# First attention: each score for the row minima issued twice in a row into its bank, with the same operands

## The reference, cut to what matters

```
Q, K, V = (x @ W.T).reshape(b, h, t, d)        # a plain reshape: b=2, h=16, t=1024, d=16
scores  = einsum('bhqd,bhkd->bhqk', Q, K), masked above the diagonal
weights = softmax(scores / sqrt(d))
ctx     = einsum('bhqk,bhkd->bhqd', weights, V)
```

## Time and profile before

| | us |
|---|---|
| three runs | 1635.82, 1642.70, 1643.36 |
| median | 1642.7 |
| the profiled execution | 1639.44 |
| its span | 1637.8 |
| first attention within the span | 233.3 to some 570 |
| TensorE busy | 1281.2 (78%) |
| VectorE busy | 895.5 (55%) |
| mean granted TensorE clock | 0.87 |

### The profile page before, as it was taken

How to read it: one execution, slowest core, us unless ns; L and a number is a source line. 1 busy time by engine, 2 the same in 40 slices (tenths; PEclk the granted TensorE clock), 3 DMA queues, 4 the chain that set the end, 5 groups by cost and what they waited for, 6 DMA issues and landing times. The chain is left out here.

```text
span 1637.8 us, 22609 instructions
## 1 busy us (share of the span) xinstructions
PE 1281.2 (78%) x7428; PEld 898.7 (55%) x7428; DVE 895.5 (55%) x2331; ACT 727.6 (44%) x1668; POOL 518.6 (32%) x556
## 2 busy tenths in 40 slices
PE   2675729889899828585899999987485999999977
PEld 2564714334344327464666666666474666666656
DVE  6645538765858243244666666650244666666640
ACT  1534404554646602443555555540334555555530
POOL 0221233332422200040555555520131554445520
PEclk8787955975959959797999999998797999999998
DMA  2313196554550086202100111005102001010005
GB/s 77 118 59 114 56 97 61 60 60 51 69 52 24 27 267 181 64 14 71 37 30 29 35 37 36 27 14 161 42 26 81 23 27 46 26 46 23 17 27 154
DMA packets 133157, 101.02 MB, mean 62 GB/s; under 512 B 48240, under 2 KB 120368, under 8 KB 132784
## 3 DMA queue, kind: packets, MB, share of 16 engines
q1 hardware_dynamic: 132000, 98.53, 26.6%
q10 hardware_dynamic: 1040, 1.05, 0.2%
HBM read 56.30 MB, written 34.87 MB: 56 GB/s over the span
## 5 line engine op out<-in xcount | busy, mean ns | idle before, releaser
L748 POOL TENSOR_SCALAR a_p<-a_p,a_rl 128x128 f32<-128x128 f32 (+7 forms) x256 | 214.9, 840 | 437.1 <-DVE a_rl L690 437.0
L731 ACT ACTIVATE a_p<-psum,a_nm 128x128 f32<-128x128 f32 (+7 forms) x256 | 189.9, 742 | 193.3 <-DVE a_nm L684 192.1
L1225 ACT ACTIVATE a_pt<-psum 128x512 f32<-128x512 f32 (+3 forms) x384 | 167.1, 492 | 148.0 <-PE psum L1098 146.2
L781 PE MATMUL psum<-ident,a_p 128*128 128x128 f32 x1152 | 186.3, 279 | 56.2 <-ACT a_pt L715 35.2
L1088 PE MATMUL psum<-a_op_k,a_op_q 64*128 64x512 f32 (+3 forms) x384 | 160.7, 511 | 51.1 <-POOL a_op_k L1023 31.7
L781 PEld LDWEIGHTS psum<-ident,a_p 128*128 128x128 f32 x1152 | 130.8, 141 | 94.1 <-ACT a_pt L715 52.5
L803 PE MATMUL psum<-a_pt,v 128*64 128x256 f32 (+1 forms) x1280 | 158.9, 370 | 2.0 <-ACT a_pt L715 2.0
L684 DVE CUSTOM_DVE_ANT_0 psum<-psum,mask_a 128x128 f32<-128x128 f32 (+3 forms) x128 | 63.8, 499 | 173.3 <-PE psum L766 173.2
L1098 PE MATMUL psum<-a_op_q,a_op_k 64*128 64x512 f32 (+3 forms) x384 | 134.8, 455 | 0.0
L1088 PEld LDWEIGHTS psum<-a_op_k,a_op_q 64*128 64x128 f32 x384 | 80.1, 236 | 87.4 <-issue 31.9
L1098 PEld LDWEIGHTS psum<-a_op_q,a_op_k 64*128 64x128 f32 x384 | 73.4, 230 | 88.9 <-ACT a_pt L1225 46.3
(11 more groups left out here) (257 smaller groups left out, 2822.6 us busy)
## 6 DMA issues: line engine op xcount, KB each, us to landing
a_swap<-a_raw SPq DMA_DIRECT2D x64, 128.0 KB, 2.3
ot_d<-a_ot SPq DMA_DIRECT2D x16, 512.0 KB, 2.6
o_ot<-ot_d SPq DMA_DIRECT2D x16, 512.0 KB, 6.3
a_raw_q<-qk_d SPq DMA_DIRECT2D x48, 128.0 KB, 5.2
a_raw_k<-qk_d SPq DMA_DIRECT2D x48, 128.0 KB, 9.2
a_wf<-wf_d SPq DMA_DIRECT2D x16, 384.0 KB, 3.3
qk_d<-p_stage_h SPq DMA_DIRECT2D x8, 512.0 KB, 2.7
qk_d<-p_stage_l SPq DMA_DIRECT2D x8, 512.0 KB, 3.4
```

The source lines that it names most:

```text
L731: e.activation(s.p[:, t % NPB, 0:(i + 1) * P], C.score[t % 2][:, 0:(i + 1) * P], ACT.Exp, scale=-1.0, bias=s.nm[:, k:k + 1], accum_out=s.l ...
L748: e.tensor_scalar(s.p[:, t % NPB, 0:(i + 1) * P], s.p[:, t % NPB, 0:(i + 1) * P], s.rl[:, k:k + 1], 1.0, ALU.mult, ALU.mult).then_inc(s.no ...
L781: ins = e.transpose(C.turn[par][:, (k - k0) * P:(k - k0 + 1) * P], s.p[:, tt % NPB, k * P:(k + 1) * P], C.ident[:, :])
L1225: e.activation(pt[:, k // G0 % NPT, hd, off:HALF], bank_b("score", g, k)[:, off:HALF], ACT.Exp, scale=-1.0).then_inc(exped, 1)
```

## The change

Every A score is issued as two matmuls in a row, with the same operands, into the same bank. Each starts a new accumulation, so the second overwrites the first with the same values. The semaphore that VectorE waits for is raised by the second.

```diff
                     free_a("score", g, k)
                     k0, k1 = w * HALF, min((w + 1) * HALF, (i + 1) * P)
-                    e.matmul(bank_a("score", g, k)[:, 0:k1 - k0], q[rows(hd), hd % 2, i * P:(i + 1) * P],
-                             kk[rows(hd), hd % 2, k0:k1], start=True, stop=True).then_inc(a_scored, 1)
+                    for _ in range(2):
+                        ins = e.matmul(bank_a("score", g, k)[:, 0:k1 - k0], q[rows(hd), hd % 2, i * P:(i + 1) * P],
+                                       kk[rows(hd), hd % 2, k0:k1], start=True, stop=True)
+                    ins.then_inc(a_scored, 1)
```

## The result

The changed kernel took 1653.6 us (median of four runs, 1650.6 to 1656.1) against 1641.2 us for the kernel before in the same comparison: a ratio of 1.008, 95% interval 1.0048 to 1.0112, or some 13 us slower. The forecast was 13.6 us faster. The profiled execution after took 1650.59 us, 11.2 us more than the one before (1639.44), and this is what the following accounts for.

A forecast was written before the change was run, and what follows sets the result against it. VectorE, 28 us busy per iteration, was taken to set the pace at full clock, TensorE at half clock. Terms -15.6 + 0.5 + 1.5 = -13.6 us on 1642.7 us gave 1629 us, range 1610 to 1668 us.

The forecast's parts named there:

- What bounds the kernel now: First attention: VectorE, 28 us busy per iteration, mostly sets the pace at full clock; TensorE does where the clock is halved.
- The cost of a duplicate: Iterations at full clock: duplicates add 8.1 us of TensorE, of which 3.8 us show above iteration 6's 33.9 us.
- What it does to the stall: TensorE's wait for GpSimd at slot 34 shrinks from 2.9 us; iterations 1 to 6 run at full clock, -15.6 us.
- the 1.1 us that the clock survives: Waits of about 1.1 us for the normalisation in iterations 3, 5 and 6, without a fall of the clock.
- the prediction's factor of 1.43: Slots 0 to 23 and 36 to 47: time at half clock over full clock, 34.8 against 24.3 us.
- Iteration 0, +1.5 us: Iteration 0, starting at half clock: slower slots but perhaps an earlier clock, +1.5 us, from -1.5 to +9 us.
- The start, +0.5 us: Iteration -1, A scores alone at half clock: duplicates mostly hidden under VectorE, +0.5 us; not hidden at all, 15 us.
- R2: Rival: the clock still falls once in iterations 1, 2 and 4; +50 us, 1692 us; chance 0.12.
- R3: Rival: one or two cold stretches left, each some 15 us above the forecast; 1650 us, 1640 to 1670; chance 0.17.
- The chance of 0.24 for slower: Whole kernel: probability given to a slower result, made of R2 and most of R3.
- The second rule of the Trainium skill: Short idle times between matmul bursts make the clock swing; set aside because 64.6 us of full clock held despite waits.

The follow-up runs named there:

- e1: Changed kernel, but with the A scores of iteration -1 issued once and only those of iterations 0 to 6 twice: 1646.1 us, ratio 1.0027.
- e0: The changed kernel run again without any further edit, in a later group: 1646.0 us, ratio 1.0057 to the kernel before.
- e3: Changed kernel with the reciprocals' turn back moved from slot 34 to 40 and the normalisation from 36 to 41: 1617.9 us, ratio 0.9868.
- e5: Changed kernel with GpSimd's second reorder held back until VectorE's first cut of the minima in iteration -1: 1642.5 us, ratio 1.0049.
- e10: Kernel before with turn back at slot 44, normalisations at 45 and 16, only A scores of at most 256 columns issued twice: 1600.6 us, ratio 0.9736.

## Why the prediction was wrong

- **What bounds the kernel now**: right. The swing between iterations with a stall and iterations at half clock is what moving the turn back and its normalisation removed, for 44 us (ratio 0.9732).
- **The cost of a duplicate, 37.7 us for an iteration at full clock**: right, with some luck in the last digit, since it was the middle between 35.8 and 39.6 us. Iterations of the changed schedule without a fall and without a stall took 37.5 (e1) and 37.4 us (e0). On schedules without the waits the difference was 3.3 and 3.4 us, where 3.8 us had been forecast.
- **What it does to the stall: the step that failed.** "The stall shrinks from 2.9 us to 0.2 to 0.5 us, well below the 1.1 us that the clock survives. [...] So iterations 1 to 6 would all run at full clock". TensorE's part was right (26.7 us against 27.1). GpSimd was ready 27.7 to 28.5 us in, where 27.6 was forecast, since its operand landed late and not always at the same point (its second reorder began 23.2 to 24.2 us into the iteration, against 22.9 and 23.0 us in iterations 1 and 4 before), and the stall was 1.0 to 1.9 us. And there was no wait of 1.1 us that the clock safely survives. The waits for `normalise` in iterations 3, 5 and 6, from which that limit was read, are 1.28 us; but in iteration 0 of the same trace the clock fell 0.28 us after such a wait of 1.29 us, and in iteration 2, at 355.3, behind one of 0.72 us. In the changed kernel the stall and the normalisation's wait of 1.2 us follow each other within 3 us, and the clock fell in 14 of 18 iterations: behind the stall where it was 1.4 us or more, behind or in the second wait where it was shorter.

  Compared with 6 x 37.45 = 224.7 us, the measured 244.6 us hold 6.4 us of stalls, and the rest, some 13 us, roughly fits the 37.5 us at half clock that the profile has there (the prediction's factor of 1.43 makes 11 us of it). The gain of the clock in iterations 1 to 5 (0.72 to 0.82 before, 0.88 to 0.96 after) and the price of the duplicates, 6 x 3.5 = 21 us, all but cancelled; iteration 6, which had the full clock before, only lost (33.9 to 40.2 us).
- **Iteration 0, +1.5 us: 2.7 us.** The full clock came back earlier, as forecast (at 271.0 instead of 280.1 us), but TensorE then waited 2.80 us for GpSimd at slot 34, where it had waited 0.35 us, and the clock fell for 10.2 us. The sum had no term for this.
- **The start, +0.5 us: mis-sized, 8.0 us.** 4.6 us of it is pace: 30.4 us (e3 and e5) with no slow VectorE instruction against 25.8. VectorE is busy 25.75 us there (e3), so it waited for scores. Nearly all of it belongs to the wide duplicates: in e10, with only the narrow ones, iteration -1 took 30.1 us with a slow subtraction of 3.64 us in it. The likely reason is that a duplicate lengthens the way from a free bank to a finished score, and that the three banks hold too little work behind two short minima of 128 columns; this was argued from the timeline, not tested. The other 3.4 us are the subtraction behind the reorder, which e5 took away.
- **The rivals.** R2 (the swing stays, 1692 us) did not happen: the long stretches of half clock are gone. What happened is nearest to R3, cold stretches left; but where R3 had one or two of 15 us' worth each, there was one in every iteration from 1 to 6, 3.4 to 10.2 us long and together worth some 13 us, with the start's 7 us on top. The chance of 0.24 for slower was carried by these two. The range reached to 1668 us, so it held the time; the sign was wrong.
- **The second rule of the Trainium skill** that the prediction weighed (TensorE: Matmul & The Clock Gate, psum-queue depth-cycling: short idle times between bursts make the clock swing) was turned down for one stretch of 64.6 us. The runs agree with it more than with the dismissal: waits of 0.4 to 2.2 us for GpSimd, the shorter ones with one of 1.2 us behind them, made the clock fall again and again.

## What to carry to other kernels

Extra matmuls that only keep TensorE busy cost time of their own, here 3.3 to 3.5 us in an iteration of 32 to 34 us, and most of the clock that they hold is to be had for nothing where a wait can be moved: six slots for one transpose, with its normalisation right behind it, were worth 2.7%, the duplicates cost 0.8%. When the forecast rests on a wait that the clock survives, look through the whole trace for a fall behind a wait of that size before you trust the limit; then look at the next wait behind it, and at the scatter of the transfer that ends it. And a slower engine moves every other engine's work in time: look for what the moved work now meets.

## What the runs showed of the hardware

- A VectorE instruction of 0.17 us took 2.9 to 3.6 us when it started under a GpSimd instruction of 3.65 us that reads and writes SBUF, and ended with it. With the GpSimd instruction held back it took 0.17 us. The Trainium skill's page SBUF — State Buffer (SBUF: two separate sides) says that the two share a pair of ports under an exclusive lock, held for the whole instruction, so that the loser blocks; the timeline agrees. It was the subtraction with two SBUF inputs in some runs and the cast with one in others.
- The same wait of 1.21 us with the same work around it let the clock fall in iteration 6 of the changed kernel's first profile and left it at 1.00 in iteration 6 of its second (e0). A single wait of this size doesn't decide it.
- With every score of kind A issued twice, the clock came back sooner. The stretches at 0.50 that began at slot 34 or later in iterations 0 to 6 lasted 3.4 to 13.7 us in the four profiles of that schedule (the changed kernel, e0, e1 and e5), against 20.5, 37.5 and 37.5 us behind the three stalls of the kernel before, in one of the longest of which TensorE was busy for 35.59 of 37.40 us all the same. The stalls were not all alike, but behind one of 2.80 us in the changed kernel the stretch was 10.2 us. What TensorE must do to get the clock back isn't shown by these runs.
- The changed kernel's 14 executions span 1641 to 1656 us over two groups, the four of e3 1614 to 1622 us: the schedule without the two waits is faster, and seems steadier.
